# One wide GpSimd instruction for the low halves of two relu blocks, in place of two

## The chip, the cores and the metric

The kernel is one program on one core of a Trainium2 chip, written for the engines directly: each engine runs its own list of instructions, and waits on semaphores where it needs another's result. The metric is the device time of one execution in microseconds (us), the median of several executions. Names of the engines in the rows: PE is TensorE's matmuls, PEld its weight loads, DVE VectorE, ACT ScalarE, POOL GpSimd, SP the queue that issues the DMAs.

## The reference, cut to what matters

The network has two parts. The first is four layers of a retention block over 8 sequences of 512 tokens and 256 features. The second, in which the change lies, is a mixture of 8 experts with two matmuls and a relu between them:

```
gates = entmax_bisect(xt @ Wr + br)
h = relu(einsum('td,edf->etf', xt, W1) + b1)
y = einsum('etf,efd->etd', h, W2) + b2
out = einsum('etd,te->td', y, gates)
x = layernorm(x + out)
```

## The kernel before

**Precision.** Every float32 matmul is made of three matmuls with operands of a reduced format, each operand split into a high half (the value rounded to that format) and a low half (what the rounding left): high x low and low x high are added to high x high. The helper `mm3` issues the three; in the rows they are lines 1559, 1560 and 1561. So whatever a matmul reads has to be made twice, as a high half and as a low half.

**The expert stage** takes the last 1404 us of the span. The 8 sequences are worked on as 4 pairs of 2 x 512 tokens. For each pair there are 32 *quads* (8 experts x 4 pieces of the hidden width), 128 quads in all. A quad is one Strassen-like step on 2 x 2 blocks of 128 x 512: seven *products* on the way up (W1) instead of eight, whose sums give four hidden blocks C11, C22, C21, C12 (k = 0 to 3), then eight `mm3` on the way down (W2), two for each block (dh = 0, 1). That is 15 `mm3`, 45 matmuls a quad.

**The hidden block.** For each quad q, block C11 goes through ScalarE alone: `relu(q, C11)` writes the high half `hid_hi` (line 918) and the full value `full` (line 921), both from PSUM. C22 and C21 are first summed by VectorE (`block_sum`, line 1355) into `full`, then ScalarE writes `hid_hi` (line 925) and the relu of `full` in place (line 926), C22 first. After each block ScalarE raises `relu_ready` by one. GpSimd makes the low half `hid_lo` of C11, C22 and C21 by a subtraction, full minus high (`low_hidden`, line 648), and raises `hid_ready`. The low half of C12 is made by VectorE (line 1360).

**TensorE's order** is written out by hand: the products of quad w + 1 alternate with the `down` steps of quad w. `down(w, k, 0)` waits until `hid_ready` has reached 3w + k + 1, that is, until the low half of block k is there:

```
elif dh == 0:
    pe.wait_ge(hid_ready, 3 * q + k + 1)
```

Between the end of product 4 of quad w + 1, on which the relu of C11 of that quad waits (`up_done`, 7q + 5), and `down(w + 1, C11, 0)`, TensorE has seven `mm3`: down C21 twice, product 5, down C12, product 6, down C12, and product 0 of quad w + 2. In certain quads it has transposes or the router's matmuls there as well: lines 1783 and 1755 (four 128-column transposes in each of 12 quads, twice), line 1765 (32 small matmuls in 3 quads), line 1772 (one transpose in 4 quads). Behind `down(w + 1, C11, 0)` come product 1 of quad w + 2, which waits for the block sum of C21 (`sums`), and later product 3, which waits for VectorE's `second_sum` (line 1342).

**GpSimd's order** for step w of the loop is: `add_expert` (line 661, from w = 4 on), the sums of the next weights (lines 626, 631 and 633, in the first 29 steps), then the low halves of quad w + 1. The low halves of the tokens of the next pair (line 643) follow in seven steps of each pair. VectorE's normalisation of the tokens and of the output (lines 1258, 1264) is put between its block sums in some quads of each pair, as are the routing steps (lines 1300 to 1334).

Of the kernel before, what the change touches and what calls it, by code (L numbers as in the profile page):

```python
# [21 lines left out]
ALU = mybir.AluOpType  # L22
# [9 lines left out]
def f32(ap):  # L32

    return ap.bitcast(F32)
# [14 lines left out]
def network(nc, x, Wkqv, Wm1, bm1, Wm2, bm2, gn_g, gn_b, Wf1, bf1, Wf2, bf2, ln_g, ln_b,  # L49
# [30 lines left out]
    h_v = h_store.rearrange("i s (k p) d -> i s p k d", p=P)  # L80

    E, _, F = W1.shape
    FP = F // (2 * P)
    QPP = E * FP
# [8 lines left out]
    C11, C22, C21, C12 = range(4)  # L93
# [8 lines left out]
    with ExitStack() as ctx:  # L102
# [3 lines left out]
        def sem(name):  # L106
            return ctx.enter_context(nc.semaphore(name))
# [51 lines left out]
        def place(name, shape, at, dt=F32):  # L159
            return nc.alloc_sbuf_tensor_at(name, shape, dt, offset=base + at)  # L160
# [41 lines left out]
        hid_hi = place("hid_hi", [P, 4, S], WORK[B_] + 12 * KB + 64, F32R)  # L202
        full = place("full", [P, 4, S], WORK[B_] + 20 * KB + 64)
        hid_lo = place("hid_lo", [P, 4, S], WORK[B_] + 28 * KB + 64, F32R)
# [62 lines left out]
        def out_bank(j):  # L267
# [11 lines left out]
        up_done, s1_ready, sums, relu_ready, hid_ready, hid_used = (  # L279
            sem(n) for n in ("up_done", "s1_ready", "sums", "relu_ready", "hid_ready", "hid_used"))  # L280
# [15 lines left out]
        def x_moments(p, t):  # L296
            return (4 * p - 2 if p else 0) + t

        def z_moments(p, t):
            return 4 * (p + 1) - (2 if p == PAIRS - 1 else 0) + t  # L300
# [264 lines left out]
        def _(pool):  # L565
# [39 lines left out]
            def layernorm_rstd(s, at):  # L605

                pool.wait_ge(z_var[s], at.base + U)
                nc.gpsimd.tensor_tensor(out=zr[s][:, 0, :], in0=zr[s][:, 0, :], in1=neg_half[:, :], op=ALU.pow).then_inc(z_rstd[s], 2)
                pool.wait_ge(z_rstd[s], at.base + 2)
                nc.gpsimd.tensor_tensor(out=zr[s][:, 1, :], in0=zr[s][:, 0, :], in1=zr[s][:, 1, :], op=ALU.mult).then_inc(z_rstd[s], 2)  # L610

            def split_f(s, at):
                for c in range(FC):
                    pool.wait_ge(f_hi[s], at.base + c + 1)
                    low_half(pf_sp[s][1][:, c, :], tmp[s][:, c, :], pf_sp[s][0][:, c, :], f_lo[s], 1)

            def sum_weights(q):
                s = q % RAWS

                def part(n):  # L620
                    return we_raw[:, s, n * P:(n + 1) * P]

                pool.wait_ge(we_raw_loaded[s], (q // RAWS + 1) * 2 * DMA)
                if q >= RAWS:
                    pool.wait_ge(w_split, q - RAWS + 1)
                nc.gpsimd.tensor_tensor(out=we_raw[:, s, 8 * P:10 * P].rearrange("p (n c) -> p n c", n=2),
                                        in0=part(0).unsqueeze(1).to_broadcast([P, 2, P]),
                                        in1=we_raw[:, s, P:3 * P].rearrange("p (n c) -> p n c", n=2),
                                        op=ALU.subtract).then_inc(w_summed, 1)
                pool.wait_ge(w_summed, 3 * q + 1)  # L630
                nc.gpsimd.tensor_tensor(out=part(10), in0=part(9), in1=part(1), op=ALU.subtract).then_inc(w_summed, 1)
                pool.wait_ge(w_summed, 3 * q + 2)
                nc.gpsimd.tensor_tensor(out=part(11), in0=part(3), in1=part(10), op=ALU.add).then_inc(w_summed, 1)

            def inverse_root(n):
                pool.wait_ge(var_ready, n + 1)
                nc.gpsimd.tensor_tensor(out=rstd[n % 2][:, :], in0=rstd[n % 2][:, :], in1=neg_half[:, :], op=ALU.pow).then_inc(rstd_ready, 1)

            def low_token(p, m):
                pool.wait_ge(t_high, 7 * p + m + 1)  # L640
                if p == 1 and m == 0:
                    pool.wait_ge(h_stored[B_], (STEPS + 1) * DMA)
                nc.gpsimd.tensor_tensor(out=te_lo[p % 2][:, m, :], in0=moving(p, m), in1=f32(te_hi[p % 2][:, m, :]),
                                        op=ALU.subtract).then_inc(t_split, 1)

            def low_hidden(q, k):
                pool.wait_ge(relu_ready, 4 * q + k + 1)
                nc.gpsimd.tensor_tensor(out=hid_lo[:, k, :], in0=full[:, k, :], in1=f32(hid_hi[:, k, :]),  # L648
                                        op=ALU.subtract).then_inc(hid_ready, 1)

            def root(p):
                pool.wait_ge(disc_ready, p + 1)
                nc.gpsimd.tensor_tensor(out=tau[:, 5, :], in0=tau[:, 4, :], in1=neg_half[:, 0:1].to_broadcast([P, NB]),
                                        op=ALU.pow).then_inc(root_ready, 1)

            def add_expert(n, j):
                at = acc[n // E % 2][:, j % 2, (j // 2) * S:(j // 2 + 1) * S]
                if n:
                    pool.wait_ge(acc_added, added(n - 1, j))
                pool.wait_ge(out_gated, 4 * n + j + 1)  # L660
                nc.gpsimd.tensor_tensor(out=at, in0=at, in1=out_scaled[:, j, :], op=ALU.add).then_inc(acc_added, 1)  # L661
# [52 lines left out]
            layernorm_rstd(A_, LAST_STEP)  # L714
            sum_weights(2)
            split_f(B_, LAST_STEP)
            for k in (C11, C22, C21):
                low_hidden(0, k)
            for w in range(QUADS):
                p, i = w // QPP, w % QPP  # L720
                if w >= 0 and p and i in (5, 7):
                    inverse_root(z_moments(p - 1, (i - 5) // 2))
                if w >= 0 and p + 1 < PAIRS and i in (11, 12):
                    inverse_root(x_moments(p + 1, i - 11))
                if w == 1:
                    root(0)
                if w == 2:
                    layernorm_rstd(B_, LAST_STEP)
                if w >= 0 and p + 1 < PAIRS and i == 24:
                    root(p + 1)  # L730
                if w >= FP:
                    add_expert(w // FP - 1, w % FP)
                if w + 3 < QPP:
                    sum_weights(w + 3)
                if w + 1 < QUADS:
                    for k in (C11, C22, C21):
                        low_hidden(w + 1, k)
                if w >= 0 and p + 1 < PAIRS and 18 <= i < 25:
                    low_token(p + 1, i - 18)
            for t in range(2):  # L740
# [1197 lines left out]
```

## Time and profile before

| | |
|---|---|
| median of 3 runs | 2596.47 us (2596.22 to 2596.80) |
| the profiled execution | 2595.91 us, its span 2594.2 us |
| mean granted clock of TensorE | 0.987 of full speed |
| expert stage, from 1190 us on | 1404 us, TensorE busy 1366.6 us of it |
| GpSimd in that stage | 790.2 us busy, 495.0 us of it in line 648 |

The span is what the trace covers; 1.7 us lie around it. A busy TensorE is one whose records leave no gap; since matmuls are pipelined, the record of one (0.39 us) is longer than the distance to the next (0.23 us).

### The profile page before, as it was taken

How to read it: one execution, taken by the hardware profiler on the slowest of the kernel's cores; microseconds unless marked ns; L12 is line 12 of the kernel's file. 1: busy time of each engine (PE TensorE's matmuls, PEld its weight loads, DVE VectorE, ACT ScalarE, POOL GpSimd, SP SyncE). 2: the span in 40 equal slices, each digit the busy share in tenths (PEclk: the TensorE clock that was granted, in tenths of full speed). 3: DMA queues.
4: the chain of work that ended last, by engine and by line, in shares of the span. 5: the costliest groups of instructions: out<-in, count | busy, mean ns of one | idle time of the engine just before them, and what ended most of it. 6: DMA issues, size and time to landing. Idle time of an engine off the chain costs nothing. (4 is left out here: it accounts for less than half of the span.)

```text
span 2594.2 us, 35492 instructions
## 1 busy us (share of the span) xinstructions
PE 2490.3 (96%) x11766; PEld 2039.3 (79%) x11766; DVE 1551.5 (60%) x2976; ACT 1372.0 (53%) x2412; POOL 1359.0 (52%) x1256
## 2 busy tenths in 40 slices
PE   7999999999999999988999999999999999999997
PEld 5788878887888778876878788788887788888886
DVE  1566666666666656677777755656546665464445
ACT  4566666666666666654545544344444444444443
POOL 2244554445444644466777864546545556444454
PEclk9999999999999999999999999999999999999999
DMA  4110111000211112014654564434445334444341
GB/s 159 62 33 32 33 39 60 28 28 18 73 32 32 33 41 66 25 64 155 209 199 166 198 215 163 166 128 144 161 167 184 126 145 144 161 151 167 143 150 69
DMA packets 104582, 283.45 MB, mean 109 GB/s; under 512 B 7024, under 2 KB 77056, under 8 KB 88064
## 3 DMA queue, kind: packets, MB, share of 16 engines
q1 hardware_dynamic: 104320, 281.75, 31.5%
q8 instruction: 69, 1.13, 0.2%
q14 instruction: 65, 0.53, 0.1%
q10 hardware_dynamic: 128, 0.03, 0.0%
HBM read 212.16 MB, written 69.60 MB: 109 GB/s over the span
## 5 line engine op out<-in xcount | busy, mean ns | idle before, releaser
L648 POOL TENSOR_TENSOR hid_lo<-full,hid_hi 128x512 fp32r<-128x512 f32 x384 | 499.3, 1314 | 592.8 <-ACT full L921 479.8
L1355 DVE SCALAR_TENSOR_TENSOR full<-ps,bias_cols,sum 128x512 f32<-128x512 f32 x384 | 288.0, 750 | 215.9 <-PE ps L1561 202.3
L1559 PE MATMUL ps<-hid_hi,m_w 128*128 128x512 f32 x1024 | 407.5, 398 | 0.2 <-ACT z L855 0.2
L1561 PE MATMUL ps<-hid_hi,m_w 128*128 128x512 f32 x1024 | 405.1, 396 | 0.0
L1560 PE MATMUL ps<-hid_lo,m_w 128*128 128x512 f32 x1024 | 404.0, 395 | 0.0
L1559 PE MATMUL ps<-te_hi,m_w 128*128 128x512 f32 x896 | 357.3, 399 | 18.9 <-DVE full L1355 12.8
L918 ACT ACTIVATE hid_hi<-ps,bias_cols 128x512 fp32r<-128x512 f32 x128 | 88.3, 690 | 510.3 <-PE ps L1561 510.3
L1560 PE MATMUL ps<-te_lo,m_w 128*128 128x512 f32 x896 | 355.4, 397 | 0.0
L1561 PE MATMUL ps<-te_hi,m_w 128*128 128x512 f32 x896 | 355.1, 396 | 0.0
L925 ACT ACTIVATE hid_hi<-full 128x512 fp32r<-128x512 f32 x256 | 161.7, 632 | 172.1 <-DVE full L1355 171.8
L580 POOL TENSOR_TENSOR pf_sp<-tmp,pf_sp 128x512 fp32r<-128x512 f32 x128 | 164.3, 1316 | 168.5 <-ACT pf_sp L842 168.5
L1559 PEld LDWEIGHTS ps<-hid_hi,m_w 128*128 128x128 f32 x1024 | 193.6, 189 | 46.4 <-issue 0.6
L1561 PEld LDWEIGHTS ps<-hid_hi,m_w 128*128 128x128 f32 x1024 | 193.3, 189 | 45.4
L1560 PEld LDWEIGHTS ps<-hid_lo,m_w 128*128 128x128 f32 x1024 | 193.4, 189 | 44.3
L1559 PEld LDWEIGHTS ps<-te_hi,m_w 128*128 128x128 f32 x896 | 169.2, 189 | 68.1 <-DVE full L1355 17.9
L1342 DVE TENSOR_TENSOR sum<-ps,sum 128x512 f32<-128x512 f32 x128 | 88.5, 691 | 207.5 <-PE ps L1561 187.2
L1561 PEld LDWEIGHTS ps<-te_hi,m_w 128*128 128x128 f32 x896 | 169.6, 189 | 39.5
L1560 PEld LDWEIGHTS ps<-te_lo,m_w 128*128 128x128 f32 x896 | 169.6, 189 | 38.6
L596 POOL TENSOR_SCALAR_AFFINE_SELECT pf_sp<-pf_sp 128x128 fp32r<-128x128 f32 x256 | 65.4, 297 | 199.0 <-DVE pf_sp L1086 199.0
L661 POOL TENSOR_TENSOR m_acc<-m_acc,out_scaled 128x512 f32<-128x512 f32 x124 | 165.6, 1335 | 0.0
L1346 DVE TENSOR_TENSOR sum<-ps,sum 128x512 f32<-128x512 f32 x128 | 88.2, 689 | 124.5 <-PE ps L1561 124.5
L926 ACT ACTIVATE full<-full 128x512 f32<-128x512 f32 x256 | 159.1, 622 | 0.0
(199 smaller groups left out, 5723.3 us busy)
## 6 DMA issues: line engine op xcount, KB each, us to landing
m_w<-prepared SPq DMA_DIRECT2D x96, 1408.0 KB, 6.0
prepared<-m_w SPq DMA_DIRECT2D x32, 1408.0 KB, 5.8
h_store<-h_out SPq DMA_DIRECT2D x32, 512.0 KB, 3.2
we_raw<-in_L_ffn_W SPq DMA_DIRECT2D x64, 256.0 KB, 6.4
gate_bc<-gate_rows SPq DMA_DIRECT2D x64, 256.0 KB, 6.3
h_in<-h_store SPq DMA_DIRECT2D x24, 512.0 KB, 4.3
h_in<-in_L_attn_x SPq DMA_DIRECT2D x8, 512.0 KB, 4.9
raw<-in_L_attn_Wf SPq DMA_DIRECT2D x8, 512.0 KB, 7.4
```

Source lines behind the costliest of these rows:

```text
L580: nc.gpsimd.tensor_tensor(out=lo, in0=full, in1=f32(hi), op=ALU.subtract).then_inc(done, n)
L648: nc.gpsimd.tensor_tensor(out=hid_lo[:, k, :], in0=full[:, k, :], in1=f32(hid_hi[:, k, :]), op=ALU.subtract).then_inc(hid_ready, 1)
L661: nc.gpsimd.tensor_tensor(out=at, in0=at, in1=out_scaled[:, j, :], op=ALU.add).then_inc(acc_added, 1)
L918: nc.scalar.activation(hid_hi[:, k, :], src, ACT.Relu, bias=bias)
L925: nc.scalar.activation(hid_hi[:, k, :], src, ACT.Relu)
L926: nc.scalar.activation(full[:, k, :], src, ACT.Relu).then_inc(relu_ready, 1)
L1342: nc.vector.tensor_tensor(out=sum2[:, :], in0=bank_b, in1=sum1[:, :], op=ALU.add).then_inc(sums, 1)
L1346: nc.vector.tensor_tensor(out=sum3[:, :], in0=bank_b, in1=sum1[:, :], op=ALU.add).then_inc(sums, 1)
L1355: nc.vector.scalar_tensor_tensor(out=full[:, k, :], in0=src, scalar=b1_col(e, 2 * fp + BLOCK_ROW[k]), in1=other[:, :], op0=ALU.add, op1=AL ...
L1559: nc.tensor.matmul(out, w[0], x[0], start=first, stop=False, skip_group_check=True)
L1560: nc.tensor.matmul(out, w[0], x[1], start=False, stop=False, skip_group_check=True)
L1561: return nc.tensor.matmul(out, w[1], x[0], start=False, stop=last, skip_group_check=True)
```

## The change

`low_hidden` now takes a range of blocks. For C11 and C22, which stand next to each other in `hid_lo`, `full` and `hid_hi`, it issues one subtraction over 2 x 512 columns, after waiting for `relu_ready` of the second of them, and raises `hid_ready` by two at its end. C21 is done as before. Nothing else is touched; the waits of the consumers stand as they were.

```diff
-            def low_hidden(q, k):
-                pool.wait_ge(relu_ready, 4 * q + k + 1)
-                nc.gpsimd.tensor_tensor(out=hid_lo[:, k, :], in0=full[:, k, :], in1=f32(hid_hi[:, k, :]),
-                                        op=ALU.subtract).then_inc(hid_ready, 1)
+            def low_hidden(q, first, stop):
+                pool.wait_ge(relu_ready, 4 * q + stop)
+                nc.gpsimd.tensor_tensor(out=hid_lo[:, first:stop, :], in0=full[:, first:stop, :], in1=f32(hid_hi[:, first:stop, :]),
+                                        op=ALU.subtract).then_inc(hid_ready, stop - first)
...
                 if w + 1 < QUADS:
-                    for k in (C11, C22, C21):
-                        low_hidden(w + 1, k)
+                    low_hidden(w + 1, C11, C22 + 1)
+                    low_hidden(w + 1, C21, C21 + 1)
```

The same pair of calls replaces the loop for quad 0. On GpSimd, in the quads of the last pair, the list of before reads as follows; `x3` are C11, C22 and C21 of one quad, and line 661 adds one expert's output to the accumulator.

```order
L661 TENSOR_TENSOR m_acc_94<-m_acc_94,out_scaled 128x512
L648 TENSOR_TENSOR hid_lo<-full,hid_hi 128x512 x3
L661 TENSOR_TENSOR m_acc_94<-m_acc_94,out_scaled 128x512
L648 TENSOR_TENSOR hid_lo<-full,hid_hi 128x512 x3
L661 TENSOR_TENSOR m_acc_94<-m_acc_94,out_scaled 128x512
```

The list of the changed kernel at the same place:

```order
L661 TENSOR_TENSOR m_acc_94<-m_acc_94,out_scaled 128x512
L648 TENSOR_TENSOR hid_lo<-full,hid_hi 128x1024
L648 TENSOR_TENSOR hid_lo<-full,hid_hi 128x512
L661 TENSOR_TENSOR m_acc_94<-m_acc_94,out_scaled 128x512
L648 TENSOR_TENSOR hid_lo<-full,hid_hi 128x1024
L648 TENSOR_TENSOR hid_lo<-full,hid_hi 128x512
```

The operand is one run of 1024 columns, and the number of GpSimd's instructions for it falls from three to two a quad, 384 to 256 in all. The lists of the other engines are the same in both kernels. TensorE's list at the place where it waits for the two low halves (`m_w_89` are the weights of quad w, `m_w_90` those of quad w + 1; `te_hi`, `te_lo` the tokens' halves) reads in both:

```order
L1559 MATMUL ps<-te_hi_97,m_w_90 128x512 [waits relu_ready,w_loaded0]
L1560 MATMUL ps<-te_lo_99,m_w_90 128x512
L1561 MATMUL ps<-te_hi_97,m_w_90 128x512
L1559 MATMUL ps<-hid_hi,m_w_89 128x512 [waits hid_ready]
L1560 MATMUL ps<-hid_lo,m_w_89 128x512
L1561 MATMUL ps<-hid_hi,m_w_89 128x512
L1559 MATMUL ps<-te_hi_97,m_w_90 128x512 [waits sums]
```

The first wait on `hid_ready` is that of `down(w, C11, 0)`; it stands where it stood, and what raises the semaphore for it is now the wide instruction. The wait for C22 comes four `mm3` later.

## Rows read from the trace of the kernel before

**Rows 1.** The page, part 1 and part 5's first group.
```profile
PE 2490.3 (96%) x11766; PEld 2039.3 (79%) x11766; DVE 1551.5 (60%) x2976; ACT 1372.0 (53%) x2412; POOL 1359.0 (52%) x1256
...
L648 POOL TENSOR_TENSOR hid_lo<-full,hid_hi 128x512 fp32r<-128x512 f32 x384 | 499.3, 1314 | 592.8 <-ACT full L921 479.8
```
**Rows 2.** Busy time of each engine in the expert stage.
```profile
1190.00:2594.00 1404.00, 1366.58 (x5934) 1100.34 (x5932) 832.06 (x1230) 639.46 (x1097) 790.20 (x630) 0.99 0.46 161
```
**Rows 3.** Waits of TensorE's weight loads, expert stage: total us, times, longest.
```profile
PEld ps L1559 <- DVE full L1355: 17.9, 12, 3.6
PEld ps L1559 <- DVE sum L1342: 8.6, 11, 1.1
...
PEld ps L1559 <- DVE sum L1346: 2.1, 3, 1.0
```
**Rows 4.** Timeline of quad 97, a regular one: start, us.
```profile
2252.51 0.68 ACT L921 ACTIVATE full<-ps,bias_cols 128x512 f32<-128x512 f32 x1
...
2253.28 2.55 POOL L648 TENSOR_TENSOR hid_lo<-full,hid_hi 128x512 fp32r<-128x512 f32 x2 [5.13 <-ACT full L921]
...
2253.61 0.63 ACT L926 ACTIVATE full<-full 128x512 f32<-128x512 f32 x1
...
2256.03 1.29 POOL L648 TENSOR_TENSOR hid_lo<-full,hid_hi 128x512 fp32r<-128x512 f32 x1 [0.20 <-ACT full L926]
...
2256.38 0.19 PEld L1559 LDWEIGHTS ps<-hid_hi,m_w 128*128 128x128 f32 x1
```
**Rows 5.** GpSimd's subtractions and sums by line: ns min/median/max.
```profile
L648 POOL TENSOR_TENSOR hid_lo<-full,hid_hi x384: 1263/1299/2293, 1177.4 to 2572.1; 128x512 fp32r<-128x512 f32 x192
L366 POOL TENSOR_TENSOR z<-z,lnv x30: 2355/2403/2418, 163.2 to 1136.6; 128x1024 f32<-128x1024 f32 x30
L580 POOL TENSOR_TENSOR h_sp<-h_in,h_sp x32: 2192/2207/2670, 22.4 to 1107.5; 128x1024 fp32r<-128x1024 f32 x32
```
**Rows 6.** Timeline of a short stall of TensorE.
```profile
1793.89 1.60 DVE L1355 SCALAR_TENSOR_TENSOR full<-ps,bias_cols,sum 128x512 f32<-128x512 f32 x2
1794.06 0.40 PE L1561 MATMUL ps<-hid_hi,m_w 128*128 128x512 f32 x1
...
1794.69 0.19 PEld L1559 LDWEIGHTS ps<-te_hi,m_w 128*128 128x128 f32 x1 [0.68 <-DVE full L1355]
1794.70 0.50 PE L1559 MATMUL ps<-te_hi,m_w 128*128 128x512 f32 x1 [0.24 <-DVE full L1355]
...
1795.03 0.40 PE L1560 MATMUL ps<-te_lo,m_w 128*128 128x512 f32 x1
1795.27 0.40 PE L1561 MATMUL ps<-te_hi,m_w 128*128 128x512 f32 x1
```
**Rows 7.** Timeline of quad 36, with transposes.
```profile
1589.02 0.63 ACT L926 ACTIVATE full<-full 128x512 f32<-128x512 f32 x1
...
1592.22 0.19 PEld L1559 LDWEIGHTS ps<-hid_hi,m_w 128*128 128x128 f32 x1
```
**Rows 8.** Timeline of quads 14 and 20.
```profile
1348.41 0.61 ACT L926 ACTIVATE full<-full 128x512 f32<-128x512 f32 x1
...
1350.99 0.19 PEld L1559 LDWEIGHTS ps<-hid_hi,m_w 128*128 128x128 f32 x1
...
1417.98 0.62 ACT L926 ACTIVATE full<-full 128x512 f32<-128x512 f32 x1
...
1419.98 0.19 PEld L1559 LDWEIGHTS ps<-hid_hi,m_w 128*128 128x128 f32 x1
```
**Rows 9.** Timeline of the last quad, 127.
```profile
2569.67 0.63 ACT L926 ACTIVATE full<-full 128x512 f32<-128x512 f32 x1
...
2571.73 0.19 PEld L1559 LDWEIGHTS ps<-hid_hi,m_w 128*128 128x128 f32 x1
```
**Rows 10.** Two operations of VectorE by line: ns min/median/max.
```profile
L1258 DVE TENSOR_SCALAR m_hs<-m_hs,m_mv,m_rstd x24: 400/408/1436, 1609.2 to 2331.2; 128x256 f32<-128x256 f32 x24
...
L1360 DVE SCALAR_TENSOR_TENSOR hid_lo<-full,hid_hi x128: 679/682/1806, 1188.8 to 2572.9; 128x512 fp32r<-128x512 f32 x128
```

More of the change, by code:

```diff
@@ L716, in _ @@
             split_f(B_, LAST_STEP)
-            for k in (C11, C22, C21):
-                low_hidden(0, k)
+            low_hidden(0, C11, C22 + 1)
+            low_hidden(0, C21, C21 + 1)
             for w in range(QUADS):
@@ L735, in _ @@
                 if w + 1 < QUADS:
-                    for k in (C11, C22, C21):
-                        low_hidden(w + 1, k)
+                    low_hidden(w + 1, C11, C22 + 1)
+                    low_hidden(w + 1, C21, C21 + 1)
                 if w >= 0 and p + 1 < PAIRS and 18 <= i < 25:
```

## The prediction

> **What bounds the kernel now.** I read the page first [rows 1]. TensorE is busy 96% of the span, and line 648, the one that changes, is GpSimd's largest group: 384 instructions, 499 us, mean 1.314 us. GpSimd stands idle 593 us before them, and it is ScalarE's line 921 that ends most of that wait. The view of busy time by stretches [rows 2] says the same of the stage where line 648 runs: TensorE 1366.6 of 1404 us, GpSimd 790. The view of waits for that stage [rows 3] tells what TensorE still waits for: block sums and other sums of VectorE, 28.6 us of late weight loads in 26 waits. GpSimd does not appear in it at all. So GpSimd's busy time is worth nothing here, and taking some of it away gives nothing by itself. What counts is the moment at which each low half is ready, against the moment at which TensorE asks for it. That slack is read from the timeline of one quad [rows 4]. Quad 97 stands for the regular ones: the distances below repeat to 0.03 us in 76 of the 128 quads.
>
> **The slack before.** In quad 97 ScalarE ends the full value of C11 at 2252.51 + 0.68 = 2253.19, and GpSimd starts at 2253.28, after 0.08 of semaphore (0.08 in nearly all quads). C11 and C22 together take 2.55 us, C11 alone 1.30, so its low half is ready at 2254.58. TensorE loads the weights of down(C11, 0) at 2256.38: 1.80 us to spare.
>
> **The change, step by step.**
> *What it removes.* One instruction a quad. The wide one costs what a flat run of 1024 columns costs on GpSimd. The trace has such rows: line 366 has a median of 2.403 and a range of 2.355 to 2.418 [rows 5]; I take 2.40. Two of 512 take 2.55, so GpSimd saves 0.15 us a quad, 19 us of busy time in all, hidden under TensorE, worth 0. The lower bound is another row of 1024 columns, 2.19 us, of line 580 (its operand is cut in four runs of 256, which the new one isn't) [rows 5]; the upper bound is that line's longest, 2.67, where VectorE was at the same memory.
> *What it adds.* The wide instruction waits for the relu of C22, and its semaphore rises only at its end, for both blocks. In quad 97 ScalarE ends C22 at 2253.61 + 0.63 = 2254.24. Start 0.08 later, 2.40 of work, 2256.72; TensorE sees it about 0.05 later. I take that 0.05 from a wait in [rows 6]: VectorE's first block sum ends at about 1793.89 + 0.75 = 1794.64, the load starts at 1794.69. So the release is at 2256.77, and the load that now starts at 2256.38 [rows 4] is **0.39 us late**. C11's 1.80 us of slack are gone: 1.05 for the wait for C22, 1.1 for its columns.
> *What 0.39 late costs TensorE.* Weight loads run one matmul ahead, so not all of it is lost. The stall in [rows 6] shows the exchange: matmuls normally follow each other at 0.23 us. The load starts 1794.69 instead of at about 1794.06 (a load starts with the matmul before its own), 0.63 late. The matmuls are 1794.06, 1794.70, 1795.03: gaps 0.64 and 0.33 instead of 0.23 and 0.23, so 0.51 are lost, then the pace is back. A load that is late by x costs x - 0.12. For x = 0.39 that is **0.27 us a quad**. It comes back in every quad: relu, low half and this load all hang on product 4 of the same quad, and a stall moves all of them together.
> *Where it does not show.* (a) In 26 quads TensorE has other work in between: 12 quads with transposes of the output, 12 of the tokens and 3 of the router, and quad 2 with its wait for the gates, less two counted below. Quad 36 is of this kind [rows 7]: release 1589.02 + 0.63 + 0.08 + 2.40 + 0.05 = 1592.18, load at 1592.22. Nothing is late: 0. Quad 0 is ready long before. (b) In 15 quads TensorE stalls right behind this load on VectorE (the 26 waits of [rows 3] fall in them, mostly line 1355, wanted one mm3 later). VectorE's work there began before the new stall, so the old stall shrinks by the new one: 0.
> *Where it costs more.* (c) In seven quads of the first pair (7, 14, 20, 21, 23, 24, 27) VectorE's sum of C22 comes late, which the old order forgave. Quad 14, the least: 1348.41 + 0.61 + 0.08 + 2.40 + 0.05 = 1351.55 against 1350.99, 0.56 late, 0.44 lost; quad 20: 1421.13 against 1419.98, 1.15 late, 1.03 lost [rows 8]. The seven make 5.2 us. (d) The last quad has no products of a next one as cover: 2569.67 + 0.63 + 2.53 = 2572.83 against 2571.73, 1.10 late, 1.0 lost [rows 9]. (e) Two quads with only the gates' transpose in between: 0.16 each, 0.3.
> *What waits behind.* On TensorE, product 1 and all that follows; it shifts with it. C22's own low half comes with C11's and is wanted four mm3, 2.8 us, later. C21's subtraction starts behind the wide one at about +0.35 instead of -0.35 against C11's load in quad 97 [rows 4] and is wanted eight mm3, 5.5 us, after that load: hidden, as is add_expert behind it.
>
> **Sum.** Quads: 76 x 0.27 = 20.5; (c) 5.2; (d) 1.0; (e) 0.3: 27.0 us.
>
> *The port.* One more thing moves. Short operations of VectorE are stretched when they meet GpSimd's: line 1258 takes 0.41 us at the median and 1.44 at most, line 1360 0.68 and 1.81 [rows 10]. The stretch, 1.0 and 1.1 us, is close to one GpSimd instruction of 1.30 [rows 5]. After the change GpSimd's port is free for a further 1.05 us (it waits for C22) and then taken for 2.40 in one piece. That can give VectorE up to 1.05 in one of the 15 quads of (b) or take up to 1.1; both signs occur, and I put it at nothing, with 8 us either way. The Trainium skill, page "SBUF — State Buffer", section "Who interferes with whom", says that GpSimd and a VectorE operation with two SBUF inputs hold a shared port as an exclusive lock for the whole instruction, so a wider one locks longer. The trace agrees as far as lines 1258 and 1360 go; nothing in it shows a lock of 2.4 us in this stage.
>
> Against the profiled execution that is 2595.91 + 27 = 2622.9, its span about 2621. The median of the runs is 0.56 above the profiled time; it becomes 2596.47 + 27 = 2623.5, and I write **2623**, 1.0% slower.
>
> **Rivals.**
> *A: as forecast*, 0.78. Own range 2612 to 2633: the port's 8, and 0.03 in the per-quad number (76 x 0.03 = 2.3).
> *B: the wide instruction is shorter than a flat one of before*, near 2.19. Then quad 97 is 0.18 late and loses 0.06: 76 x 0.06 + (5.2 - 7 x 0.21) + 0.8 = 9 us, 2606. For it: line 580. Against it: the 30 flat instructions of line 366 all lie between 2.355 and 2.418. 0.06.
> *C: the wide instruction is held back or holds VectorE back*. If VectorE is caught for 1.1 us more (2.40 instead of 1.30) in each of the 15 stalling quads: +16, 2640. Or if TensorE's lead doesn't help here and each late load costs its full 0.39: 76 x 0.12 = +9, 2633. For it: the 2.29 maximum of line 648 and 2.67 of line 580 [rows 5]. Against: in regular quads VectorE does only block sums from PSUM in that time. By the page's rule this one would be the more likely outcome in the stalling quads. 0.07.
> *D: TensorE's clock.* It is granted at 0.99 in this stage [rows 2]. If the small gaps made it fall more often, each fall would cost 16 matmuls at 0.43 instead of 0.23, 3 us; ten of them +30, 2653. The stall of [rows 6], larger than the new ones, is followed by matmuls at the old pace. 0.02.
> *E, the other side: the release is in time.* Decisive point: the wide instruction must be 2.40 - 0.27 = 2.13 us or shorter, at GpSimd in the second half of quad 97. Then 76 quads lose nothing, the seven lose 5.2 - 7 x 0.27 = 3.3, (d) 0.7, and VectorE's free port can give back some of 28.6 us of stalls [rows 3]: 2596 to 2600 at the least, or faster. No row of 1024 columns is below 2.19. 0.07, of which 0.03 faster and 0.04 within 0.2%.
> That the change doesn't do what it says is excluded by the lists: the wide operand is there in every quad.
>
> **Numbers.** 0.2% of this time is 5.2 us, about what a measurement can tell. Slower by more: A, B, C and D, 0.93; within it 0.04; faster 0.03. The range takes A whole, and reaches on the low side to B's 2606 halfway, 2608, and on the high side to the first half of C, 2636; left out are E, half of B, half of C and D.
>
> **What the changed profile would show.** Line 648 in two forms, x128 of 128x1024 at 2.40 us and x128 of 512 at 1.3. In the waits a new line, weight loads of line 1559 waiting for POOL line 648, about 100 times, some 40 us by loads and about 27 by matmuls. The distance between regular quads 10.7 us instead of 10.4 (45 matmuls at 0.23), that of quads with transposes unchanged. VectorE's waits a little shorter than 28.6. It would be wrong if the wide instruction is below 2.2, if the loads' lateness is not 0.39, or if the stalls behind VectorE change by more than 8 us.

## The result and the profile after

The changed kernel takes **2626.03 us** (median of 4 runs, 2625.38 to 2629.26) against 2596.64 us for the kernel before (4 runs, 2596.22 to 2598.97): ratio 1.0114, 95% interval 1.0099 to 1.0129. It is 29.4 us slower; 26.5 were forecast (2623 against 2596.5). The profiled execution took 2625.38 us, 29.5 more than that of before.

The page of the changed kernel, part 1, the chain that ended last, and the first group of part 5:

```profile
PE 2511.7 (96%) x11766; PEld 2030.8 (77%) x11766; DVE 1523.5 (58%) x2976; ACT 1372.3 (52%) x2412; POOL 1339.4 (51%) x1128
...
PE 27%; POOL 7%; ACT 4%; issue 3%; DVE 1%; POOLq 0%; DVEq 0%
...
L648 POOL TENSOR_TENSOR hid_lo<-full,hid_hi 128x1024 fp32r<-128x1024 f32 (+1 forms) x256 | 473.4, 1868 | 645.4 <-ACT full L926 645.4
```

GpSimd is busy 20 us less than in [rows 1], as the change intends, and 7% of the chain now runs over it. Its wait is no longer ended by ScalarE's line 921 (the value of C11) but by line 926 (the relu of C22). The two shapes of line 648 in the expert stage, by the view that keeps shapes apart (busy us, mean ns of one, idle before):

```profile
L648 POOL TENSOR_TENSOR hid_lo<-full,hid_hi 128x1024 fp32r<-128x1024 f32 x127 | 310.0, 2441 | 596.8 <-ACT full L926 596.8
L648 POOL TENSOR_TENSOR hid_lo<-full,hid_hi 128x512 fp32r<-128x512 f32 x127 | 164.6, 1296 | 45.3 <-ACT full L926 45.3
```

The waits of TensorE's weight loads in the same stage, the view of [rows 3]:

```profile
PEld ps L1559 <- POOL hid_lo L648: 59.1, 100, 1.8
PEld ps L1559 <- DVE full L1355: 8.5, 8, 3.5
...
PEld ps L1559 <- DVE sum L1342: 5.6, 6, 1.1
...
PEld ps L1559 <- DVE sum L1346: 1.8, 3, 1.0
```

A line that before did not have is now the largest: 100 loads wait for GpSimd. VectorE's three lines fall from 28.6 to 15.9 us. And quad 97, the place of [rows 4]:

```profile
2273.87 0.63 ACT L926 ACTIVATE full<-full 128x512 f32<-128x512 f32 x1
...
2274.64 3.67 POOL L648 TENSOR_TENSOR hid_lo<-full,hid_hi 128x1024 fp32r<-128x1024 f32 x2 [5.88 <-ACT full L926]
...
2276.66 0.40 PE L1561 MATMUL ps<-te_hi,m_w 128*128 128x512 f32 x1
...
2277.11 0.19 PEld L1559 LDWEIGHTS ps<-hid_hi,m_w 128*128 128x128 f32 x1 [0.49 <-POOL hid_lo L648]
2277.11 0.51 PE L1559 MATMUL ps<-hid_hi,m_w 128*128 128x512 f32 x1
...
2277.45 0.39 PE L1560 MATMUL ps<-hid_lo,m_w 128*128 128x512 f32 x1
```

The relu ends at 2274.50 and GpSimd starts at 2274.64. Its row joins the wide and the narrow instruction; the wide one takes 2.41. The load is 0.49 late, and the matmuls at 2276.66, 2277.11 and 2277.45 lie 0.45 and 0.34 apart instead of 0.23 and 0.23: 0.33 lost here. The picture is the predicted one with a somewhat larger number.

To say where the 29 us lie, I take the distance from one quad's C11 load to the next, after minus before, for quads 1 to 127. It adds up to 28.6; a further 0.85 us lies outside, 0.97 ahead of quad 0's load and -0.12 behind that of the last quad. Here and below, "half clock" is a stretch in which the profile's granted clock of TensorE is 0.5: in quad 45 of before 14 matmuls take 6.8 us, where at 0.23 they take 3.2. Each kernel has one trace, and such stretches lie in other quads from trace to trace, so a quad that differs by 1.5 to 3 us can differ by them alone.

| quads | count | us |
|---|---|---|
| regular, 0.25 to 0.45 each (median 0.345) | 73 | +25.9 |
| others at 0.45 to 0.52 each | 12 | +5.8 |
| 44 and 45 together (+1.6, -5.9) | 2 | -4.3 |
| 76 and 77 together (+1.6, -3.6) | 2 | -1.9 |
| 41, 73, 105, each behind one at +0.5 | 3 | -0.9 |
| 2, 6, 7, 13, 14, 19, 23 and 27, all of the first pair | 8 | +5.0 |
| 18, 50 and 82, routing steps; 3.4 us at half clock in 18 and 82 before, in 50 after | 3 | -1.9 |
| the last quad | 1 | +1.0 |
| all others, mostly quads with transposes | 23 | -0.1 |

So the loss is one small stall in each regular quad, and something else, not forecast, gives a few us back at 44/45 and 76/77. A part of that is the clock: from quad 1 on, 20.4 us are at half clock in the trace of before (6.8 of them in quad 45), 13.6 in that of the changed kernel.

### The profile page after: what moved, and what is told of

It reads as the page before. It is cut to its first block and busy times, and to the rows that moved or that the text cites. A ratio compares the mean times of both kernels' runs of the same rounds, so it can differ in the third digit from the quotient of the medians.

```text
span 2623.7 us, 35492 instructions
## 1 busy us (share of the span) xinstructions
PE 2511.7 (96%) x11766; PEld 2030.8 (77%) x11766; DVE 1523.5 (58%) x2976; ACT 1372.3 (52%) x2412; POOL 1339.4 (51%) x1128
## 5 line engine op out<-in xcount | busy, mean ns | idle before, releaser
L648 POOL TENSOR_TENSOR hid_lo<-full,hid_hi 128x1024 fp32r<-128x1024 f32 (+1 forms) x256 | 473.4, 1868 | 645.4 <-ACT full L926 645.4
L1559 PE MATMUL ps<-hid_hi,m_w 128*128 128x512 f32 x1024 | 417.7, 408 | 15.8 <-POOL hid_lo L648 9.1
L1561 PE MATMUL ps<-hid_hi,m_w 128*128 128x512 f32 x1024 | 404.6, 395 | 0.0
```

The source lines that it names most:

```text
L648: nc.gpsimd.tensor_tensor(out=hid_lo[:, first:stop, :], in0=full[:, first:stop, :], in1=f32(hid_hi[:, first:stop, :]), op=ALU.subtract).th ...
L1559: nc.tensor.matmul(out, w[0], x[0], start=first, stop=False, skip_group_check=True)
L1561: return nc.tensor.matmul(out, w[1], x[0], start=False, stop=last, skip_group_check=True)
```

## The experiments

The change does three things at once: C11's low half waits for C22's relu (the *wait*), comes with a longer instruction (the *width*), and rises in a step of two (the *count*). The lateness in quads 90 to 96, median, for each kernel (us; "late" is the gap between two weight loads over the usual 0.23):

| kernel | relu of C22 to GpSimd's start | C11's instruction(s) | load late | a regular quad |
|---|---|---|---|---|
| before | starts 0.96 before its end | 1.30 | 0.00 | |
| after | 0.143 | 2.41 | 0.49 | +0.345 |
| e1, wait alone | 0.078 | 1.30 | 0.00 | 0.00 |
| e7, 896 columns | 0.077 | 2.13 | 0.145 | 0.00 |
| e6, 768 columns | 0.077 | 1.86 | 0.00 | 0.00 |
| e3, count of one | 0.078 | 2.41 | 0.40 | +0.28 |
| e2, C22 ahead of C11 | 0.078 | 2.55 | 0.54 | +0.41 |

### e1: the wait alone

Three instructions of 512 as before, but C11's also waits for the relu of C22.

```diff
-                pool.wait_ge(relu_ready, 4 * q + k + 1)
+                pool.wait_ge(relu_ready, 4 * q + max(k, C22) + 1)
```

> Two instructions of 512 columns as before, but both wait for the relu of C22; C11 goes first. This is the wait of the change without its width. Theory A (lateness: only the moment at which C11's low half is released counts, and a load that is late by x costs x - 0.12): C11 is released 0.6 us before its load in a regular quad, no weight load waits for GpSimd, and the 29.4 us of the change are gone. Theory P (port): GpSimd leaves the port free for 1.05 us more after C11's relu, VectorE's line 1258 and 1264 run unstretched as in the changed kernel, and the stalls behind VectorE shrink; then the time is under the one before, 2586 to 2592. A without P: 2596. Rival W (waiting for the second relu costs by itself, whatever the width): 2610 or more.

Measured: 2596.84 us (11 runs) against 2597.91 (16), ratio 0.9995 (0.9986 to 1.0004). Regular quads change by 0.00. TensorE's loads for GpSimd's low halves wait in five places only:

```profile
PEld ps L1559 <- DVE full L1355: 14.4, 9, 4.6
...
PEld ps L1559 <- DVE sum L1342: 4.5, 5, 1.1
PEld ps L1559 <- POOL hid_lo L648: 3.3, 5, 1.2
```

The wait for C22 takes 1.05 us out of C11's slack of 1.80 and costs nothing where 0.76 are left. Theory P's 2586 to 2592 did not come; the time is that of A without P. But the sum hides opposite things: quads 2, 13, 23 and 25 of the first pair get 2.3, 1.9, 1.2 and 1.2 longer and quad 50 3.15, 44 and 45 together 4.0 shorter, quad 18 1.55, 76 and 77 1.7 shorter. Much of that is the clock: this trace has 6.8 us at half clock in quads 2 and 13 (3.4 each before), 3.4 in 23 (none), 6.8 in 50 (none), and none in 18 (3.4) and 45 (6.8). The give-back of the changed kernel is here as well: it belongs to the wait, not to the width.

### e2: the wait and the time, without the width

As e1, and C22's instruction goes first, so that C11's low half comes 0.08 + 2.55 us after C22's relu. C11's consumers wait for the count that C11 now reaches.

```diff
-                    for k in (C11, C22, C21):
+                    for k in (C22, C11, C21):
...
-                    pe.wait_ge(hid_ready, 3 * q + k + 1)
+                    pe.wait_ge(hid_ready, 3 * q + max(k, C22) + 1)
```

> Two instructions of 512 columns, both after the relu of C22, C22 first and C11 second: the width is undone, the lateness is kept and made greater. Theory A: the pair takes 2.55 instead of 2.41, the wait sits in the instruction (0.08 instead of 0.14), so the load of C11 is later than in the changed kernel by about 0.08, and at the same exchange each of some 90 quads loses 0.08 more: 2626 + 7 = 2633. Rival W2 (the wide form is what costs): 2596 to 2600.

Measured: 2633.84 us (4 runs), ratio 1.0145 (1.0129 to 1.016), as theory A gave it; the load is 0.54 late, a regular quad 0.41 longer.

```profile
PEld ps L1559 <- POOL hid_lo L648: 68.3, 116, 1.9
```

The slowdown of the changed kernel comes about with no wide instruction at all; what costs is the moment at which C11's low half is released.

### e3: the changed kernel, counting by one

The wide instruction raises `hid_ready` by one, and every consumer waits for the smaller count.

```diff
-                                        op=ALU.subtract).then_inc(hid_ready, stop - first)
+                                        op=ALU.subtract).then_inc(hid_ready, 1)
...
-                    pe.wait_ge(hid_ready, 3 * q + k + 1)
+                    pe.wait_ge(hid_ready, 2 * q + max(k, C22))
```

> The changed kernel, but the wide instruction raises the semaphore by one instead of two, and the consumers count two a quad. In the changed kernel the wait for the relu stands in an instruction of its own, and the wide one starts 0.14 us after the relu; with an increase of one the wait can stand in the instruction itself, as before, with 0.08. Theory A: some 100 loads are 0.06 less late: about 6 us less, 2620. Rival (the 0.14 comes from the width, for example its set-up, or from the value waited for): no difference, 2626.

Measured: 2623.13 us (4 runs, 2618.03 to 2625.21), ratio 1.0103 (1.0088 to 1.0119). It is 2.9 us below the changed kernel, half of the 6 expected, and the intervals overlap, so the times alone do not show the difference; the trace does: over the regular quads the loss falls from 0.345 to 0.28. A regular quad in it, near 2225 us:

```profile
2225.07 0.63 ACT L926 ACTIVATE full<-full 128x512 f32<-128x512 f32 x1
2225.78 3.66 POOL L648 TENSOR_TENSOR hid_lo<-full,hid_hi 128x1024 fp32r<-128x1024 f32 x2 [5.81 <-ACT full L926]
...
2228.24 0.19 PEld L1559 LDWEIGHTS ps<-hid_hi,m_w 128*128 128x128 f32 x1 [0.44 <-POOL hid_lo L648]
```

The start is back at 0.08 after the relu's end (2225.70) and the stall 0.05 to 0.09 shorter. In the trace of the changed kernel the wide subtraction carries no wait of its own: an instruction ahead of it, from the line of the wait, does the waiting. In this kernel wait and subtraction are one instruction, as before.

### e4: the width alone

In the last three pairs C11's low half is written twice, by one instruction of 1024 columns that starts where the old one did; TensorE reads the first copy, nobody the second.

```diff
+                if k == C11 and q >= QPP:
+                    out = lo_twice[:, :, :]
+                    in0, in1 = (t.unsqueeze(1).to_broadcast([P, 2, S]) for t in (full[:, k, :], f32(hid_hi[:, k, :])))
```

> The width without the wait: in the last 96 quads C11's instruction takes 2 x 512 columns (its own difference written twice, the second copy to a place nobody reads) right after C11's relu; C22 and C21 as before. GpSimd does 96 x 1.1 us more. Theory A: C11 is ready 0.7 us before its load, C22, wanted 2.8 us later, at +0.6; nothing is late: 2596 to 2600. Theory P: the port is taken without a break from C11's relu on, VectorE's stretched operations are stretched more, by up to 1.1 us each in some six quads: up to +6, 2602. Rival W2 (the wide form costs 0.3 a quad wherever it stands): 2620.

Measured: 2606.37 us (5 runs), ratio 1.0035 (1.0022 to 1.0049), above what either theory gave. Regular quads: 0.00. Quads 41, 55, 73, 87 and 105 grow by 1.15 each, 59 and 91 by 0.6, and 77 by 3.2: its stall behind VectorE lasts 4.76 instead of 3.61, and the other 2.05 go with 6.8 us at half clock behind it, of which before has none. Quad 45's stall grows as much (4.74 instead of 3.60), but it has 3.4 us at half clock instead of 6.8 and comes out at -0.2. Quad 50 grows by 1.6, with 3.4 us at half clock and no longer stall. Except for quad 50, these are quads in which TensorE stalls behind VectorE, and its waits there grow (line 1360 here is the block sum, 1355 before; 17.9 us in [rows 3]):

```profile
PEld ps L1564 <- DVE full L1360: 27.5, 14, 4.8
PEld ps L1564 <- DVE sum L1347: 8.3, 10, 1.1
```

What makes VectorE late is seen in one of its normalisations (line 1263 here, 1258 before), in the timeline:

```profile
1629.23 2.45 POOL L654 TENSOR_TENSOR lo_twice<-full,hid_hi 128x1024 fp32r<-128x1024 f32 x1 [2.05 <-ACT full L926]
1629.26 4.53 DVE L1263 TENSOR_SCALAR m_hs<-m_hs,m_mv,m_rstd 128x256 f32<-128x256 f32 x4
```

Four operations of 0.41 take 4.53 us. They issue 0.03 us behind GpSimd's instruction, and the first of them ends only when that one does; the next meeting costs another 1.0. The longest such operation was 1.44 in [rows 10]; in this kernel, by its lines:

```profile
L1263 DVE TENSOR_SCALAR m_hs<-m_hs,m_mv,m_rstd x24: 401/408/2581, 1606.6 to 2339.8; 128x256 f32<-128x256 f32 x24
```

The stretch, 2581 - 408 = 2.17 us, is GpSimd's instruction of 2.46 less 0.29; before it was 1.03 for 1.30, less 0.27. VectorE's operation is held for about what is left of GpSimd's instruction, at both widths. The Trainium skill, page "SBUF — State Buffer", section "Who interferes with whom", states that whoever issues first gets the shared ports for its whole instruction and the other blocks fully, and the trace agrees. The prediction applied the section's case of two SBUF inputs; this operation reads one SBUF tensor, and for it the section has another case, a two-port mode that `tensor_scalar` can enter. No view here shows in which mode it ran.

### e5: C22 and C21 together instead

The changed kernel, but the wide instruction takes the later two blocks; C11's stays narrow and early.

```diff
-                    low_hidden(w + 1, C11, C22 + 1)
-                    low_hidden(w + 1, C21, C21 + 1)
+                    low_hidden(w + 1, C11, C11 + 1)
+                    low_hidden(w + 1, C22, C21 + 1)
```

> The wide instruction takes C22 and C21 instead of C11 and C22; C11 goes alone and early. As many instructions and columns as in the changed kernel. Theory A: C11 is on time; C22 is released at about +2.1 us after C11's load, 0.6 before its own, so regular quads lose nothing. Where VectorE makes C21 late (the stalls of line 1355, some 8 to 12 quads), C22 is now late behind it, up to 1.6 us each: +5 to +15, 2602 to 2612. Rival W2 (the wide form costs in every quad): 2620 or more.

Measured: 2608.23 us (4 runs) against 2597.6 (21), ratio 1.0045 (1.0029 to 1.006).

```profile
PEld ps L1559 <- POOL hid_lo L648: 27.6, 23, 1.8
PEld ps L1559 <- DVE full L1355: 12.0, 7, 2.7
```

Regular quads: 0.00. The loss is in single places: quads 7 and 25 grow by 1.7 and 1.2, 20, 55 and 87 by 0.8 to 0.9, and 1.4 lie behind the last quad's load. Quads 18, 50 and 82 grow by 1.6, 3.1 and 1.6, but there the clock is at half for 6.8 us each, against 3.4, 0 and 3.4 before; quad 45, which has 6.8 us of it before, has none here (44 and 45 together -1.7). Where blocks are paired decides more than that they are paired; but no pairing of whole blocks that I tried is free.

### e6 and e7: the cut at 768 and at 896 columns

Two instructions a quad as in the change, but the first takes C11 and half (e6) or three quarters (e7) of C22, the second the rest with C21.

```diff
+                flat = [t[:, :, :].rearrange("p k n -> p (k n)") for t in (hid_lo, full, hid_hi)]
+                cut = S + 256
+                at = slice(0, cut) if part == 0 else slice(cut, 3 * S)
+                pool.wait_ge(relu_ready, 4 * q + (C22, C21)[part] + 1)
+                nc.gpsimd.tensor_tensor(out=flat[0][:, at], in0=flat[1][:, at], in1=f32(flat[2][:, at]),
+                                        op=ALU.subtract).then_inc(hid_ready, part + 1)
```

> Two instructions for the three blocks, of 768 columns each: C11 with the first half of C22 after C22's relu, the rest of C22 with C21 after C21's relu. Theory A: the first takes about 1.85 us and ends 0.15 before C11's load; no loss in regular quads. Theory P: the port is free as in the changed kernel, which gives VectorE back some of its stalls; C22 late behind C21 in a few quads takes some. Together 2590 to 2600. Rival W2: 2615.

> As with 768, but cut at 896: the first instruction takes 2.13 us, which is the break-even that the prediction names. Theory A: C11's load is late by 0.12 to 0.13, inside the lead of 0.12 that a load has, so the loads wait in nearly all quads, but the matmuls lose next to nothing: within 3 us of the 768 cut, 2590 to 2602. If there is no such lead and each late load costs its full lateness: 12 us more than the 768 cut.

Measured: e6 2597.49 us (11 runs), ratio 1.0 (0.9991 to 1.0009); e7 2597.93 (11), ratio 1.0004 (0.9995 to 1.0013); before 2597.6. Both equal to before. For e7 the waits and its first instruction by shape (line 651 here):

```profile
PEld ps L1562 <- POOL hid_lo L651: 36.2, 104, 1.5
```

```profile
L651 POOL TENSOR_TENSOR hid_lo<-full,hid_hi 128x896 fp32r<-128x896 f32 x127 | 276.7, 2179 | 560.9 <-ACT full L929 560.9
```

104 weight loads wait for GpSimd, 36 us in all, and the kernel is no slower: in regular quads the load is 0.145 late at a median of 2.13 us of work, and the quad is not longer. That is the break-even of rival E, 2.13 us, met almost exactly, and the plainest evidence that a load has a lead of some 0.14 us before its lateness costs anything.

### e8: the wait alone, in the later pairs

e1's loss lay in the first pair, its gain in the others. So:

```diff
-                pool.wait_ge(relu_ready, 4 * q + k + 1)
+                pool.wait_ge(relu_ready, 4 * q + (max(k, C22) if q >= QPP else k) + 1)
```

> As e1 (two instructions of 512 columns, C11 first, both after the relu of C22), but only from the second pair on (quads 32 to 127); the first pair as before. Theory P: in e1's trace VectorE's line 1258 is no longer stretched in the quads from 40 on, and quads 41, 45, 73, 77 and 105 are shorter by 0.6, 4.0 (with 44), 0.6, 1.7 (with 76) and 0.6 us, while quads 2, 13, 23 and 25 of the first pair are longer by 2.3, 1.9, 1.2 and 1.2. Without the first pair's losses 5 to 7 us are gained: 2590 to 2593 where the kernel before has 2597.6. Rival (the differences in those quads are falls of TensorE's clock that come and go from run to run, and the port is worth nothing in the sum): 2596 to 2598.

Measured: 2593.89 us (11 runs, 2591.34 to 2594.68) against 2597.62 (15), ratio 0.9985 (0.9976 to 0.9994), 3.7 us faster than before and the best of all versions, 0.9 above the range of theory P. Quads 44 and 45 give 4.0, 76 and 77 1.7, 41, 73 and 105 0.6 each; 55 and 87 take 0.3 each, and quad 50 takes 3.15. That one is the clock, at half in this kernel (the third number from the right is the granted clock) and at full in before:

```profile
1742.50:1749.30 6.80, 6.80 (x21) 5.64 (x21) 0.81 (x2) 1.15 (x2) 2.53 (x3) 0.51 0.00 0
```

Quad 45 is the reverse, 6.8 us at half clock in before and none here, so that most of the 4.0 is clock as well and the two about cancel. Is the whole gain then the clock, as the rival says? The granted clock of the runs says no: its mean over the 11 is 0.9869, over the 15 of before 0.9867, which is some 0.6 us of 2594. What is left is VectorE: from quad 32 on, TensorE's weight loads wait 6.0 us for it instead of 12.2, and 1.4 for GpSimd. The reason is seen in VectorE's groups of line 1258 in the expert stage, in the kernel before:

```profile
L1258 DVE TENSOR_SCALAR m_xs<-m_xs,m_mv,m_rstd 128x256 f32<-128x256 f32 x24 | 14.7, 674 | 0.0
L1258 DVE TENSOR_SCALAR m_hs<-m_hs,m_mv,m_rstd 128x256 f32<-128x256 f32 x24 | 14.3, 658 | 0.0
```

and in this one:

```profile
L1258 DVE TENSOR_SCALAR m_xs<-m_xs,m_mv,m_rstd 128x256 f32<-128x256 f32 x24 | 10.7, 510 | 0.0
...
L1258 DVE TENSOR_SCALAR m_hs<-m_hs,m_mv,m_rstd 128x256 f32<-128x256 f32 x24 | 8.3, 409 | 0.0
```

The same 48 operations take 10.0 us less: GpSimd, which now starts a microsecond later, is mostly not running when they come. The timeline of before at quads 44 and 45 shows one such meeting and its price:

```profile
1674.19 2.61 POOL L648 TENSOR_TENSOR hid_lo<-full,hid_hi 128x512 fp32r<-128x512 f32 x2 [1.94 <-ACT full L921]
1674.21 3.39 DVE L1258 TENSOR_SCALAR m_xs<-m_xs,m_mv,m_rstd 128x256 f32<-128x256 f32 x4
...
1681.54 0.29 PEld L1559 LDWEIGHTS ps<-te_hi,m_w 128*128 128x128 f32 x1 [3.60 <-DVE full L1355]
```

and the timeline of the changed kernel at the same quads:

```profile
1687.83 1.38 DVE L1258 TENSOR_SCALAR m_xs<-m_xs,m_mv,m_rstd 128x256 f32<-128x256 f32 x4
...
1689.12 1.22 DVE L1264 TENSOR_TENSOR m_xs<-m_xs,m_hs 128x1024 f32<-128x1024 f32 x1
1689.21 3.35 POOL L648 TENSOR_TENSOR hid_lo<-full,hid_hi 128x1024 fp32r<-128x1024 f32 x1 [2.75 <-ACT full L926]
...
1692.62 0.19 PEld L1559 LDWEIGHTS ps<-hid_hi,m_w 128*128 128x128 f32 x1 [1.76 <-POOL hid_lo L648]
```

Four operations take 1.38 us instead of 3.39, VectorE is 2 us earlier, and TensorE's stall of 3.60 behind it is gone; now it is GpSimd that comes second and is held behind line 1264 (3.35 us instead of 2.41), which costs a stall of 1.76. Behind the long stall of before the clock was granted at half for 6.8 us; behind the shorter one it was not. The view of busy time by stretches, of before and then of the changed kernel:

```profile
1680.80:1687.60 6.80, 6.06 (x14) 4.79 (x15) 4.52 (x7) 2.15 (x4) 3.71 (x3) 0.50 0.16 66
```

```profile
1692.60:1699.40 6.80, 6.62 (x27) 4.96 (x28) 6.25 (x11) 2.63 (x5) 3.71 (x3) 1.00 0.42 176
```

## Why the prediction held, point by point

**Where the time goes: held.** TensorE asks for C11's low half at a fixed place of each quad, and the wait for C22 (1.05) and the further columns (1.1) together use up 1.80 us of slack; either alone does not (e1 and e4: regular quads 0.00). Rival E's point, 2.13 us, is where e7 stands, and e7 loses nothing.

**The exchange x - 0.12: held.** Late by 0.145, 0.40, 0.49 and 0.54 cost 0.00, 0.28, 0.345 and 0.41: the lead takes 0.12 to 0.145 each time.

**0.39 us late in quad 97: 0.49 measured, the term mis-sized.** Of the terms the wide instruction was right (2.40; 2.41 measured), the 0.05 to TensorE too (0.051). The step that failed is "Start 0.08 later": it is 0.143, since the wait stands in an instruction of its own; e3 takes that back and gets 0.078, 0.40 late and 0.28 a quad, against 0.39 and 0.27 forecast. So 76 x 0.27 = 20.5 should have been 76 x 0.345 = 26.2, 5.7 us more. That the wait becomes its own instruction is in the changed kernel's list; the price was not in a row of before. The remaining 0.02 to 0.03 us of lateness in the changed kernel was not traced further.

**(a) Transposed quads 0: held**, within 0.05 in quad 36 and most others. Twelve quads lost 0.45 to 0.52 instead of about 0.345 or 0. Three of them, 40, 72 and 104, stand before a stalled quad and get half of it back there. Quads 3, 51, 71 and 83 follow a quad in which this load is not late, and their load shifts by its whole lateness: 0.46 to 0.48 here, 0.38 to 0.41 in e3 and 0.12 to 0.13 in e7, where a load is 0.49, 0.40 and 0.145 late. For the other five I have no experiment.

**(b) Stalled quads 0: only in part.** The new stall does come out of the old one where the old one stands, but not whole: quads 40 and 41 together still grow by 0.18, 54 and 55 by 0.76. What the step left out is that VectorE's work itself moves, below.

**(c) The seven late quads 5.2: 1.75 measured.** Quads 7, 14, 20, 21, 23, 24 and 27 changed by -0.1, -0.8, +0.1, +0.4, +1.5, +0.5 and +0.25. The step took VectorE's lateness in them from the old trace and held it fixed. But each stall ahead of them gives VectorE time to come out of its backlog, as (b) says itself; the two steps did not agree with each other. That reading is argued from the timeline; no run tests it alone.

**(d) The last quad 1.0: held**, +1.02. **(e) The two quads with the gates' transpose 0.3:** 59 and 91 measure 0.22 and 0.53, 0.75 together.

**The port at nothing, with 8 us either way: about what was measured, by parts that the step did not have.** Two things were run together there. Width does what was feared: e4 costs 8.5 us (2606.37 - 2597.91), by its trace 9.2 as longer stalls behind VectorE in nine quads, some 2 as clock, and 3.1 less ahead of the stage, where the edit changes nothing. The later start does what was hoped in the last three pairs, where e8 gains 3.7, but not in the first, since e1, which has it everywhere, shows no gain clear of the noise. In the changed kernel the start is later *and* the instruction wider, and in the last three pairs the start decides: the 48 normalisations take 18.5 us there, 29.0 before and 34.8 in e4. Together 44/45 and 76/77 gave 6.2 us back, of which I estimate some 3 as the 6.8 us at half clock that quad 45 was spared (an equal stretch in quad 50 of e8 costs 3.15); in the first pair quads 2, 6, 13, 19 and 23 took 5.7, in part by 3.4 us more at half clock in quad 2, and quad 18, spared 3.4 us of it, gave 1.7. Whether a meeting happens could have been looked for in each of the 15 quads of the old timeline, by shifting GpSimd's row by 1.05 us; that this would have given the sign is argued, not tried.

**The signs.** Distance 10.78 us between regular quads (10.7 forecast); 100 waits of line 1559 for line 648 (about 100); 59 us by loads instead of 40, of which the larger lateness explains 10 and the rest are single long ones like that of 1.76. VectorE's waits fell by 12.7 us, not "a little". Rival C, that the wide instruction holds VectorE back, is real (e4) but did not decide here; D is refuted, the clock of the expert stage was 0.99 as before, with less time at half.

So that the total was met to 3 us is in part luck. The mechanism, a late load in each regular quad, is shown; around it errors of opposite sign met. By the traces: quads of the table's first two rows that aren't of (c), 30.8 us in 83 quads where 20.5 in 76 and 0.3 in (e) were forecast, +10.0 (5.7 of it the lateness in 76); (c) -3.4; all else in the stage, VectorE's stalls and the clock, about -5 where nothing was forecast, some 3 of it clock; and +0.85 outside the stage. That makes the 2.5 by which the profiled execution exceeds the forecast 27.0.

## What to carry to other kernels

Merging two instructions of an engine that isn't the bound saves nothing and delays the first result by the wait for the second's input plus the second's length; read the consumer's slack for the *first* result, and merge only what fits in it (768 or 896 columns here, not 1024). Before putting a step of one instruction down at its own length, look for what shares a port with it: moving GpSimd's start by 1 us in the last three pairs, with nothing else changed, gained 3.7 us, while the 20 us of GpSimd's time that the change saved lie hidden under TensorE; moved in all four pairs (e1), the gain does not stand clear of the noise. And where two steps of an estimate speak of the same lateness, let both move when one does.

## What the runs showed of the hardware

- A semaphore raised by two by the same instruction that has to wait: the wait goes to a separate instruction ahead of it, and the start comes 0.143 us after the releaser's end instead of 0.078 (changed kernel against e1, e3, e6 and e7). The price goes with the instruction that raises by two, not with the wide form or the block: in e5 the one for C22 and C21 starts 0.142 behind C21's relu, and in e6 and e7, whose first instruction raises by one, so does the second where it waits at all (0.142 in quads 0 to 2).
- GpSimd's subtraction of two float32 operands: 1.30 us for 512 columns, 1.86 for 768, 2.13 for 896, 2.41 for 1024, so about 2.17 ns a column and 0.19 us besides.
- A VectorE operation of 0.41 us that comes just behind GpSimd's takes up to 1.44 when that one has 512 columns and up to 2.58 when it has 1024.
- A weight load late by 0.145 us costs TensorE nothing, by 0.49 us 0.345.
- A stretch of 6.8 us at half clock costs about 3.15 us (quad 50 of e1, e5 and e8), one of 3.4 about 1.5 (quad 50 of the changed kernel and of e2, e4 and e7). In the kernel before, as run for these comparisons, single executions ranged from 2592.3 to 2599.8 us, the six with a mean clock of 0.989 or 0.990 at 2593.9 in the mean and the 29 with 0.985 or 0.986 at 2597.9, so the clock is at least part of it. The 3.7 us of e8 were told from zero with 11 and 15 runs.
